# Attention times values for two batches in one run, in the first cross-attention of a six-phase kernel

## The chip, the cores and the metric

The kernel runs on one core of a Trainium2 chip as a single program. The metric is the device time of that program in microseconds, the median over its executions. It has five engines: TensorE (PE; its weight loads are listed as PEld), VectorE (DVE), ScalarE (ACT), GpSimd (POOL) and SyncE (SP), which issues the DMAs. All arithmetic in the stage treated here is in 32-bit floating point.

## The reference

A perceiver block of two layers on x (128 batches, 32 queries, 128 channels) and a context (128 batches, 257 keys, 128 channels). Each layer is cross-attention, self-attention and a feed-forward part, each with a layer norm before it and a residual sum after it. The change touches the first cross-attention only:

```python
q = split_heads(queries @ Wq + bq)      # 16 heads of 8 channels
k = split_heads(keys @ Wk + bk)
v = split_heads(values @ Wv + bv)
scores = jnp.einsum('bhqd,bhkd->bhqk', q, k) / jnp.sqrt(jnp.float32(HD))
scores = jnp.where(mask, jnp.float32(-1000000000000000.0), scores)
attn = jax.nn.softmax(scores, axis=-1)
ctx = jnp.einsum('bhqk,bhkd->bhqd', attn, v)
return ctx.reshape(b, sq, d) @ Wo + bo
```

The mask differs by batch. Queries are the normalised x, keys and values are both the context.

## The kernel before, in words

The six phases follow each other, each closed by a barrier. The first cross-attention is `phase_xattn0`. It prepares weights, query projections and the part of the last key (the 257th, held apart), and then walks over the 128 batches, one per **step**. A step g runs different stages of several batches, as a software pipeline written out by hand on each engine; `s.on(lag)` says whether batch g - lag exists. The first eight and last eight steps are unrolled, the others are a loop (`Fori`) of 8 steps per iteration, r = 0 to 7. The remainder r chooses the buffers. Engines meet through semaphores alone, each counting batches.

TensorE in step g (order of the code, `step` in the tensor block): scores of batch g (L552; four matmuls, one on each band of 32 rows of the array, to four PSUM banks); the projections of K (L529) and V (L534) for batch g+1 from the transposed context `cT`; at r % 4 = 1 the fold of the last key's part (L600); at r % 4 = 2 the output projection of a tile of four batches (L611, L613); the transposes of the probabilities of batch g-1, in two pairs of heads groups (L562, `turn_probs`); the transposes of the context of batch g+2 (L523, `turn`); the spread of the reciprocal sums of batch g-2 (L586, `spread_sums`); and attention times values for batch g-2 (L574, `values`): eight matmuls that the compiler issues as 16, side by side on four bands of 32 columns.

ScalarE in step g: the exponentials of batch g-1 (L684, four, each with a sum), the copies of K (L668) and V (L672) of batch g+1 out of PSUM, the copy of the first pair of transposed probabilities of g-1 (L692), the copy of the spread reciprocals of g-2 (L697, into `RS`). VectorE: masking and maximum of batch g (L731), the reciprocal (L751), the copy of the second pair of transposed probabilities (L755), the copy of the transposed context of g+2 (L719, `turned`), and the scaling of the result of `values` by `RS` into `OM` (L763). GpSimd prepares the mask and the block query of batch g+1 and small factors (L434 to L463). SyncE loads masks and context and stores the transposed context for the second layer (L408, L413).

The PSUM bank `b_vo` holds the projection of V in its first 256 columns and the result of `values` in the next 128; so the projection waits for the scaling of the batch before (`om_ok`), and `values` waits for the copy of V (`v_ev`). `V` has four buffers, `PT` (transposed probabilities) two, `RS` two. K's projection waits for the context copy of the step before (`ct_ev`), the second pair's transposes for all four exponentials (`e_ok`). In the listing, `one` and `run` set up a step; `fours` gives the tile number of a lag.

Of the kernel before, what the change touches and what calls it, by code (L numbers as in the profile page):

```python
# [19 lines left out]
ALU = mybir.AluOpType  # L20
# [5 lines left out]
P = 128  # L26
B = 128
SQ = 32
D = 128
# [272 lines left out]
def phase_xattn0(nc, sh, ctx_rows, mask, wq, bq, wk, bk, wv, bv, wo, bo):  # L302
    SCALE = HD0 ** -0.5
    with ExitStack() as ctx:
# [15 lines left out]
        Qb = sb("a_Qb", [D, 2, 4, SQ])  # L320
        cT = sb("a_cT", [D, 4, LAST])
        KT = sb("a_KT", [D, 2, SK])
        V = sb("a_V", [P, 4, 2, D])
        SM = sb("a_SM", [P, 2, 4, SK])
        PR = sb("a_PR", [P, 2, 4, SK])
        mx = sb("a_mx", [P, 2, 4])
# [5 lines left out]
        XL = sb("a_XL", [P, 2, 2 * BPT, 4, 4])  # L332
        LT = sb("a_LT", [P, BPT, SQ])
        VB = sb("a_VB", [P, 2, D])
        PT = sb("a_PT", [P, 2, 4, 2, P])
        RS = sb("a_RS", [P, 2, P])
        OM = sb("a_OM", [P, 2, 4, BPT, SQ])
        head4 = sb("a_head4", [D, 4])
# [35 lines left out]

        def run(eng, step, extra):

            def one(g, r, tile, fours):
                s = Step(g, r, B)
                s.tile, s.fours = tile, fours
                step(s)  # L380
            for g in range(8):
                one(g, g, g // 4, lambda lag, g=g: (g + lag) // 4)
            with eng.Fori(1, B // 8 - 1) as j:
                for r in range(8):
                    one(8 * j + r, r, 2 * j + r // 4, lambda lag, j=j, r=r: 2 * j + (r + lag) // 4)
            for g in range(B - 8, B + extra):
                one(g, g % 8, g // 4, lambda lag, g=g: (g + lag) // 4)

        @block.sync
        def _(sp):  # L390
# [106 lines left out]
        def _(pe):  # L497
# [25 lines left out]
                    last = nc.tensor.transpose(b_ck[:, c * P:(c + 1) * P], C[:, buf, c, :], sh.ident[:, :])  # L523
                last.then_inc(ct_ps, 1)

            def project(i, r):

                wait(pe, ct_ev, i + 1)
                nc.tensor.matmul(b_ck[:, LAST:2 * LAST], wk_s[:, :], cT[:, r % 4, :], start=True, stop=True  # L529
                                 ).then_inc(k_ps, 1)  # L530
                wait(pe, om_ok, i - 3)
                wait(pe, v_ev, i)
                for c in range(2):
                    last = nc.tensor.matmul(b_vo[:, c * D:(c + 1) * D], cT[:, r % 4, c * P:(c + 1) * P], wv_s[:, :],  # L534
                                            start=True, stop=True)
                last.then_inc(v_ps, 1)
# [27 lines left out]
                last.then_inc(pt_ps, 1)  # L564

            def values(s):
                g, v, par = s.g, (s.r - 2) % 4, s.r % 2
                wait(pe, pt0_ev, g - 1)
                wait(pe, pt1_ev, g - 1)
                wait(pe, v_ev, g + 2 if s.on(-1) else B)  # L570
                wait(pe, om_ok, g - 2)
                for c in range(2):
                    for hg in range(4):
                        last = nc.tensor.matmul(b_vo[32 * hg:32 * hg + 32, 2 * D:2 * D + P],  # L574
                                                V[:, v, c, 32 * hg:32 * hg + 32], PT[:, par, hg, c, :],
                                                start=(c == 0), stop=(c == 1), tile_position=(0, 32 * hg))
                last.then_inc(av_ps, 1)

            def spread_sums(s):

# [9 lines left out]
            def step(s):  # L590
                g, r = s.g, s.r
                if s.on(0):
                    scores(s)
                if s.on(-1):
                    project(g + 1, r + 1)
                if r % 4 == 1 and s.on(5):
                    wait(pe, x2_ok, 4 * s.fours(-5) + 4)
                    if s.on(0):
                        wait(pe, s_mx, 4 * g + 2)
                    nc.tensor.matmul(b_s[1][:, SPARE:SPARE + SQ],  # L600
                                     XL[:, (r - 5) // 4 % 2, :, :, :], sh.fold[:, :],
                                     start=True, stop=True).then_inc(l_ps, 1)
                if r % 4 == 2 and s.on(6):
                    wait(pe, om_ok, 4 * s.fours(-6) + 4)
                    wait(pe, l_ev, s.fours(-6) + 1)
                    pe.wait_ge(vb_in[(r - 6) // 4 % 2], s.values)
                    if s.on(0):
                        wait(pe, s_mx, 4 * g + 1)
                    tp = (r - 6) // 4 % 2
                    for h in range(4):  # L610
                        nc.tensor.matmul(b_s[0][:, SPARE:SPARE + D], OM[:, tp, h, :, :], wo_s[:, :],  # L611
                                         start=(h == 0), stop=False)
                    nc.tensor.matmul(b_s[0][:, SPARE:SPARE + D], LT[:, :, :], VB[:, tp, :], start=False, stop=True  # L613
                                     ).then_inc(y_ps, 1)
                if s.on(1):
                    turn_probs(s, 0)
                    turn_probs(s, 1)
                if s.on(-2):
                    turn(g + 2, (r + 2) % 4, s.ctx)
                if s.on(2):  # L620
                    spread_sums(s)
                    values(s)

            def one(g, r, tile, fours):
                s = Step(g, r, B)
                s.tile, s.fours = tile, fours
                s.ctx = 16 * (fours(2) + 1)
                s.values = 16 * (1 + (g - 6) // 8)
                step(s)

            turn(0, 0, 16)
            project(0, 0)
            turn(1, 1, 16)
            for g in range(8):
                one(g, g, g // 4, lambda lag, g=g: (g + lag) // 4)
            with pe.Fori(1, B // 8 - 1) as j:
                for r in range(8):
                    s = Step(8 * j + r, r, B)
                    s.tile, s.fours = 2 * j + r // 4, lambda lag, j=j, r=r: 2 * j + (r + lag) // 4
                    s.ctx = 32 * j + 16 * ((r + 2) // 4 + 1)  # L640
                    s.values = 16 * j if r < 6 else 16 * j + 16
                    step(s)
# [4 lines left out]
        def _(act):  # L647
# [17 lines left out]
            def project(i, r):  # L665
                wait(act, k_ps, i + 1)
                wait(act, s_ps, 4 * (i - 1))
                nc.scalar.activation(KT[:, r % 2, 0:LAST], b_ck[:, LAST:2 * LAST], ACT.Identity, bias=bias[:, 1:2]  # L668
                                     ).then_inc(k_ev, 1)
                wait(act, v_ps, i + 1)  # L670
                wait(act, av_ps, i - 3)
                nc.scalar.activation(V[:, r % 4, :, :].rearrange("p a d -> p (a d)"), b_vo[:, 0:2 * D],  # L672
                                     ACT.Copy).then_inc(v_ev, 1)

            def step(s):
                g, r = s.g, s.r
                par = r % 2
                if s.on(1):
                    wait(act, pt_ps, 2 * (g - 2))
                    wait(act, x2_ok, g - 2)  # L680
                    wait(act, rd_ok, g - 2)
                    wait(act, s_nmx, g)
                    for hg in range(4):
                        nc.scalar.activation(PR[:, 1 - par, hg, :], SM[:, 1 - par, hg, :], ACT.Exp,  # L684
                                             bias=nmx[:, 1 - par, hg:hg + 1],
                                             accum_out=den[:, 1 - par, hg:hg + 1]).then_inc(e_ok, 1)
                if s.on(-1):
                    project(g + 1, r + 1)
                if s.on(1):
                    wait(act, pt_ps, 2 * (g - 1) + 1)  # L690
                    wait(act, av_ps, g - 2)
                    nc.scalar.activation(PT[:, 1 - par, 0:2, :, :].rearrange("p a b c -> p (a b c)"), b_pt[0][:, :],  # L692
                                         ACT.Copy).then_inc(pt0_ev, 1)
                if s.on(2):
                    wait(act, r_ps, g - 1)
                    wait(act, om_ok, g - 3)
                    nc.scalar.activation(RS[:, par, :], b_s[2][:, SPARE:SPARE + P], ACT.Copy).then_inc(r_ev, 1)  # L697

            project(0, 0)
# [3 lines left out]
        def _(dve):  # L703
# [17 lines left out]
            def step(s):  # L721
# [29 lines left out]
                    nc.vector.reciprocal(rden[:, 1 - par, :], den[:, 1 - par, :]).then_inc(rd_ok, 1)  # L751
                if s.on(1):
                    wait(dve, pt_ps, 2 * g)
                    wait(dve, av_ps, g - 2)
                    nc.vector.tensor_copy(PT[:, 1 - par, 2:4, :, :].rearrange("p a b c -> p (a b c)"), b_pt[1][:, :]  # L755
                                          ).then_inc(pt1_ev, 1)
                if s.on(-2):
                    turned(g + 2, (r + 2) % 4, 16 * s.fours(2))
                if s.on(2):
                    wait(dve, av_ps, g - 1)  # L760
                    wait(dve, r_ev, g - 1)
                    wait(dve, y_ps, s.fours(-2) - 1)
                    nc.vector.tensor_tensor(OM[:, (r - 2) // 4 % 2, :, (r - 2) % 4, :],  # L763
                                            b_vo[:, 2 * D:2 * D + P].rearrange("p (h q) -> p h q", h=4),
                                            RS[:, par, :].rearrange("p (h q) -> p h q", h=4), ALU.mult).then_inc(om_ok, 1)

            turned(0, 0, 0)
            turned(1, 1, 0)
# [1873 lines left out]
```

## Time and profile before

| | us |
|---|---|
| median of 3 runs | 2544.7 |
| lowest, highest | 2540.48, 2546.29 |
| the profiled execution, its own time | 2540.67 |
| its span in the profile | 2538.9 |
| TensorE, VectorE, ScalarE, GpSimd busy in the span | 2126.7, 1645.4, 1443.1, 461.7 |
| granted TensorE clock, mean over the span | 0.922 |

The stage with the loop over batches lies between about 50 and 559 us of the span. A line of the profile names the engine, the source line and the tiles (output <- inputs, buffer numbers left out). "PE" times include the filling and emptying of the array, so neighbouring matmuls overlap in the listing; the distance between starts tells the pace. "Idle before" is the time in which that engine stood still in front of an instruction, followed by what ended it; "issue" there means that nothing the profile shows was waited for.

### The profile page before, as it was taken

Reading aid. Unit: us, or ns where it says so; the run is one execution under the profiler, and the core shown is the slowest. Engines: PE = TensorE matmul, PEld = TensorE weight load, DVE = VectorE, ACT = ScalarE, POOL = GpSimd, SP = SyncE. Lnnn points to the kernel's source line nnn. Section 1 sums busy time; section 2 is a strip of 40 time slices with the busy share of each in tenths; the row PEclk is TensorE's granted clock in tenths of the full one; section 3 lists DMA queues with packets and bytes.
Section 4 is the critical chain, followed back from the end, with each engine's and each line's share of the span. In section 5 each row is a group of like instructions: output and inputs, shape, how many; then the busy total and the mean of one; then the engine's idle time right before and its main releaser. Section 6 shows DMA issues by size and latency. Waiting matters only on the chain. (4 is left out here: it accounts for less than half of the span.)

```text
span 2538.9 us, 79619 instructions
## 1 busy us (share of the span) xinstructions
PE 2126.7 (84%) x26048; PEld 1642.3 (65%) x26087; DVE 1645.4 (65%) x5552; ACT 1443.1 (57%) x3655; POOL 461.7 (18%) x1109
## 2 busy tenths in 40 slices
PE   5999999988749997899999999996555035499998
PEld 3888888867636665899999999995144024344444
DVE  4777777776744444777787777786988888510110
ACT  4888888876612223555555555554777568522221
POOL 2555555533213331000000000000000120000000
PEclk9999999999959999999999999997988555799999
DMA  3222222210100001655555565552000000100001
GB/s 87 81 77 77 77 77 77 78 44 1 27 0 0 0 0 36 143 127 114 114 114 118 126 124 113 112 116 72 0 1 0 0 2 3 47 1 0 0 0 33
DMA packets 257633, 140.90 MB, mean 55 GB/s; under 512 B 40176, under 2 KB 255616, under 8 KB 257152
## 3 DMA queue, kind: packets, MB, share of 16 engines
q1 hardware_dynamic: 257536, 139.61, 23.5%
q8 instruction: 60, 0.98, 0.2%
q14 instruction: 37, 0.30, 0.0%
HBM read 118.57 MB, written 20.97 MB: 55 GB/s over the span
## 5 line engine op out<-in xcount | busy, mean ns | idle before, releaser
L1070 ACT ACTIVATE c_PR<-c_PR,c_nmx 128x257 f32<-128x257 f32 x512 | 252.7, 496 | 70.0 <-DVE c_nmx L1117 70.0
L1113 DVE CUSTOM_DVE_ANT_0 c_PR<-c_b,c_MB 128x257 f32<-128x257 f32 x512 | 194.9, 423 | 127.2 <-PE c_b L993 120.4
L684 ACT ACTIVATE a_PR<-a_SM,a_nmx 128x257 f32<-128x257 f32 x512 | 253.4, 500 | 4.0 <-POOL a_XL L459 3.6
L1004 PE MATMUL c_b<-c_PT,c_C 32*128 32x128 f32 x8192 | 239.3, 272 | 3.4 <-DVE c_PT L1130 2.1
L1004 PEld LDWEIGHTS c_b<-c_PT,c_C 32*128 32x128 f32 x8192 | 232.4, 187 | 7.5 <-issue 3.7
L993 PE MATMUL c_b<-c_cT,c_QP 128*128 128x257 f32 x1024 | 230.6, 383 | 1.3 <-ACT c_QP L1063 0.8
L731 DVE CUSTOM_DVE_ANT_0 a_SM<-a_bs,a_MB 128x257 f32<-128x257 f32 x512 | 188.0, 423 | 61.2 <-PE a_bs L552 33.5
L993 PEld LDWEIGHTS c_b<-c_cT,c_QP 128*128 128x128 f32 x1024 | 191.8, 190 | 32.1 <-issue 2.7
L1130 DVE STREAM_TRANSPOSE c_PT<-c_PR 128x256 f32<-128x256 f32 x512 | 181.3, 412 | 0.0
L1075 ACT ACTIVATE c_OT<-c_b 128x512 f32<-128x512 f32 x128 | 76.5, 598 | 168.8 <-PE c_b L1004 168.8
L2552 DVE TENSOR_TENSOR g_YS<-g_b,g_s 128x512 f32<-128x512 f32 x8 | 5.5, 692 | 224.2 <-PE g_b L2509 224.2
L1125 DVE TENSOR_SCALAR c_PR<-c_PR,c_rden 128x257 f32<-128x257 f32 x512 | 146.2, 351 | 4.5
L961 POOL TENSOR_TENSOR c_XL<-quarter,c_PR 128x16 f32<-128x16 f32 x128 | 27.8, 217 | 664.6 <-DVE c_PR L1125 664.6
L2520 ACT ACTIVATE g_A<-g_b,g_S 128x512 f32<-128x512 f32 x64 | 44.0, 687 | 170.7 <-PE g_b L2484 170.7
L562 PE MATMUL a_bp<-ident,a_PR 128*128 128x128 f32 x1024 | 134.5, 274 | 1.7 <-ACT a_PR L684 1.4
L2229 PE MATMUL d_bv<-d_WQ,d_HQ 128*128 128x512 bf16 x33 | 20.7, 633 | 129.0 <-PEq L2079 101.0
L978 PE MATMUL c_b<-c_XNT,c_A 128*128 (+1 forms) x1024 | 123.9, 280 | 5.7 <-POOL c_VB L967 5.7
L1023 PEld LDWEIGHTS c_b<-c_B,c_OT 128*128 128x128 f32 x1024 | 116.7, 192 | 15.9 <-DVE c_mx L1113 13.6
L1023 PE MATMUL c_b<-c_B,c_OT 128*128 128x128 f32 x1024 | 122.8, 278 | 4.5 <-DVE c_mx L1113 3.1
L978 PEld LDWEIGHTS c_b<-c_XNT,c_A 128*128 128x128 f32 x1024 | 118.8, 194 | 6.6 <-POOL c_VB L967 6.5
L1063 ACT ACTIVATE c_QP<-c_b 128x512 f32<-128x512 f32 x128 | 75.8, 597 | 76.5 <-PE c_b L978 76.5
L562 PEld LDWEIGHTS a_bp<-ident,a_PR 128*128 128x128 f32 x1024 | 117.0, 144 | 3.1 <-ACT a_PR L684 3.1
(487 smaller groups left out, 4923.8 us busy)
## 6 DMA issues: line engine op xcount, KB each, us to landing
c_C<-in_ctx_dram SPq DMA_DIRECT2D x512, 128.0 KB, 3.2
a_C<-in_ctx_dram SPq DMA_DIRECT2D x128, 128.0 KB, 2.1
ctxT_dram<-a_cT SPq DMA_DIRECT2D x128, 128.0 KB, 1.8
c_cT<-ctxT_dram SPq DMA_DIRECT2D x128, 128.0 KB, 3.3
a_MK<-in_mask_Bx1xSxS_bk_dram SPq DMA_DIRECT2D x128, 32.1 KB, 1.9
X<-in_x_dram SPq DMA_DIRECT2D x4, 512.0 KB, 6.2
g_h<-in_L_ffn_h_w_dram SPq DMA_DIRECT2D x2, 1024.0 KB, 8.3
out_dram<-X SPq DMA_DIRECT2D x1, 2048.0 KB, 8.7
```

What stands on the lines that cost most here:

```text
L562: last = nc.tensor.transpose(b_pt[pair][:, (2 * k + c) * P:(2 * k + c + 1) * P], PR[:, par, 2 * pair + k, c * P:(c + 1) * P], sh.ident[:, :])
L684: nc.scalar.activation(PR[:, 1 - par, hg, :], SM[:, 1 - par, hg, :], ACT.Exp, bias=nmx[:, 1 - par, hg:hg + 1], accum_out=den[:, 1 - par, h ...
L731: nc.vector.tensor_tensor_reduce(SM[:, par, hg, :], b_s[hg][:, 0:SK], MB[:, par, :], 1.0, NEG1, ALU.add, ALU.max, mx[:, par, hg:hg + 1]).t ...
L978: last = nc.tensor.matmul(banks[:, c, i * P:(i + 1) * P], A[:, 4 * c + i, :], sh.XNT[:, ds(tile * P, P)], start=True, stop=True)
L993: nc.tensor.matmul(banks[:, hg, 0:SK], QP[:, s.r, b, 4 * hg:4 * hg + 4, :], cT[:, buf, :], start=True, stop=True).then_inc(s_ps, 1)
L1004: last = nc.tensor.matmul(banks[:, h, 0:P], C[rows, b, kb, :], PT[rows, b, kb, :, :], start=(kb == 0), stop=(kb == NKB - 1), tile_position ...
L1023: nc.tensor.matmul(second[:, 0, 0:D], OT[:, par, h, :, :], BH[:, h, :], start=(h == 0), stop=False)
L1070: nc.scalar.activation(PR[:, b, hg, :], PR[:, b, hg, :], ACT.Exp, bias=nmx[:, b, hg:hg + 1], scale=SCALE, accum_out=den[:, b, hg:hg + 1]). ...
L1075: nc.scalar.activation(OT[:, par, :, b, :].rearrange("p (a h) q -> p h a q", h=4), banks[:, :, 0:P].rearrange("p h (a q) -> p h a q", a=4) ...
L1113: nc.vector.tensor_tensor_reduce(PR[:, b, hg, :], banks[:, hg, 0:SK], MB[:, :], 1.0, NEG1, ALU.add, ALU.max, mx[:, b, hg:hg + 1]).then_inc ...
L1125: nc.vector.tensor_scalar(PR[:, b, hg, :], PR[:, b, hg, :], rden[:, b, hg:hg + 1], None, ALU.mult).then_inc(n_ok, 1)
L1130: nc.vector.transpose(PT[:, b, :, hg, :], PR[:, b, hg, 0:LAST]).then_inc(t_ok, 1)
```

## The change

`values` is called in odd steps only (r % 2 = 1), and then for batches g-3 and g-2 one after the other: its output takes 256 columns of `b_vo` instead of 128, and the whole bank is then in use. VectorE scales both with one operation, which reads both buffers of `RS`. `om_ok` now counts pairs of batches, so that every wait on it is rewritten with `pairs(lag)` = (g + lag) // 2. `V` gets eight buffers for four and `PT` four for two, and the waits on `av_ps` that guard them are later by four and by two batches. The spread of the reciprocals stays in every step.

```diff
-        V = sb("a_V", [P, 4, 2, D])
+        V = sb("a_V", [P, 8, 2, D])
-        PT = sb("a_PT", [P, 2, 4, 2, P])
+        PT = sb("a_PT", [P, 4, 4, 2, P])
...
-            def project(i, r):
+            def project(i, r, pairs):
...
-                wait(pe, om_ok, i - 3)
+                wait(pe, om_ok, pairs)
...
             def values(s):
-                g, v, par = s.g, (s.r - 2) % 4, s.r % 2
+                g, r = s.g, s.r
                 wait(pe, pt0_ev, g - 1)
                 wait(pe, pt1_ev, g - 1)
                 wait(pe, v_ev, g + 2 if s.on(-1) else B)
-                wait(pe, om_ok, g - 2)
-                for c in range(2):
-                    for hg in range(4):
-                        last = nc.tensor.matmul(b_vo[32 * hg:32 * hg + 32, 2 * D:2 * D + P],
-                                                V[:, v, c, 32 * hg:32 * hg + 32], PT[:, par, hg, c, :],
-                                                start=(c == 0), stop=(c == 1), tile_position=(0, 32 * hg))
-                last.then_inc(av_ps, 1)
+                wait(pe, om_ok, s.pairs(-3))
+                for i in range(2):
+                    v, p = (r - 3 + i) % 8, (r - 3 + i) % 4
+                    for c in range(2):
+                        for hg in range(4):
+                            last = nc.tensor.matmul(b_vo[32 * hg:32 * hg + 32, 2 * D + i * P:2 * D + (i + 1) * P],
+                                                    V[:, v, c, 32 * hg:32 * hg + 32], PT[:, p, hg, c, :],
+                                                    start=(c == 0), stop=(c == 1), tile_position=(0, 32 * hg))
+                    last.then_inc(av_ps, 1)
...
-                    project(g + 1, r + 1)
+                    project(g + 1, r + 1, s.pairs(-2))
...
-                    wait(pe, om_ok, 4 * s.fours(-6) + 4)
+                    wait(pe, om_ok, 2 * s.fours(-6) + 2)
...
                 if s.on(2):
                     spread_sums(s)
+                if r % 2 == 1 and s.on(2):
                     values(s)
...
-                wait(act, av_ps, i - 3)
-                nc.scalar.activation(V[:, r % 4, :, :].rearrange("p a d -> p (a d)"), b_vo[:, 0:2 * D],
+                wait(act, av_ps, i - 7)
+                nc.scalar.activation(V[:, r % 8, :, :].rearrange("p a d -> p (a d)"), b_vo[:, 0:2 * D],
...
-                    wait(act, av_ps, g - 2)
-                    nc.scalar.activation(PT[:, 1 - par, 0:2, :, :].rearrange("p a b c -> p (a b c)"), b_pt[0][:, :],
+                    wait(act, av_ps, g - 4)
+                    nc.scalar.activation(PT[:, (r - 1) % 4, 0:2, :, :].rearrange("p a b c -> p (a b c)"), b_pt[0][:, :],
...
-                    wait(act, om_ok, g - 3)
+                    wait(act, om_ok, s.pairs(-2))
...
-                    wait(dve, av_ps, g - 2)
-                    nc.vector.tensor_copy(PT[:, 1 - par, 2:4, :, :].rearrange("p a b c -> p (a b c)"), b_pt[1][:, :]
+                    wait(dve, av_ps, g - 4)
+                    nc.vector.tensor_copy(PT[:, (r - 1) % 4, 2:4, :, :].rearrange("p a b c -> p (a b c)"), b_pt[1][:, :]
...
-                if s.on(2):
+                if r % 2 == 1 and s.on(2):
+                    b = (r - 3) % 4
                     wait(dve, av_ps, g - 1)
                     wait(dve, r_ev, g - 1)
                     wait(dve, y_ps, s.fours(-2) - 1)
-                    nc.vector.tensor_tensor(OM[:, (r - 2) // 4 % 2, :, (r - 2) % 4, :],
-                                            b_vo[:, 2 * D:2 * D + P].rearrange("p (h q) -> p h q", h=4),
-                                            RS[:, par, :].rearrange("p (h q) -> p h q", h=4), ALU.mult).then_inc(om_ok, 1)
+                    nc.vector.tensor_tensor(OM[:, (r - 2) // 4 % 2, :, b:b + 2, :],
+                                            b_vo[:, 2 * D:2 * D + 2 * P].rearrange("p (b h q) -> p h b q", b=2, h=4),
+                                            RS[:, :, :].rearrange("p b (h q) -> p h b q", h=4), ALU.mult
+                                            ).then_inc(om_ok, 1)
```

## Rows read from the trace of the kernel before

**Rows 1.** Busy time by stretch: the stage, and one iteration of its loop.

```profile
core 0: us, PE busy (x) PEld busy (x) DVE busy (x) ACT busy (x) POOL busy (x), PEclk, DMA share, GB/s
52.00:548.00 496.00, 494.29 (x5490) 397.08 (x5489) 395.13 (x1728) 432.83 (x1508) 258.86 (x659) 1.00 0.27 77
269.82:301.54 31.72, 31.66 (x353) 25.51 (x353) 25.22 (x111) 27.59 (x97) 16.49 (x43) 1.00 0.26 77
```

**Rows 2.** Waits, 100 to 500 us: us in total, times, longest us.

```profile
PEld a_bck L529 <- issue: 33.4, 100, 0.3
ACT a_PT L692 <- PE a_bp L562: 28.5, 38, 1.0
...
PEld a_bs L552 <- issue: 21.7, 101, 0.3
...
ACT a_RS L697 <- PE a_bs L586: 17.7, 100, 0.2
```

**Rows 3.** Timeline of TensorE, spread to spread in a plain step: start, duration, line.

```profile
285.04 0.27 PE L586 MATMUL a_bs<-ident,a_m 128*128 128x128 f32 x1
...
285.24 0.65 PE L574 MATMUL a_bvo<-a_PT,a_V 128*32 128x128 f32 x16
...
285.81 0.76 PE L552 MATMUL a_bs<-a_KT,a_Qb 32*128 32x257 f32 x8
...
286.50 0.70 PE L529 MATMUL a_bck<-a_cT,a_wk 128*128 128x256 f32 x2
...
287.03 0.61 PE L534 MATMUL a_bvo<-a_wv,a_cT 128*128 128x128 f32 x4
...
287.48 1.04 PE L562 MATMUL a_bp<-ident,a_PR 128*128 128x128 f32 x8
...
288.35 0.38 PE L523 MATMUL a_bck<-ident,a_C 128*128 128x128 f32 x2
...
288.57 0.27 PE L586 MATMUL a_bs<-ident,a_m 128*128 128x128 f32 x1
```

**Rows 4.** Timeline of VectorE and ScalarE around the first of these spreads.

```profile
285.02 0.69 DVE L755 COPY a_PT<-a_bp 128x512 f32<-128x512 f32 x1
...
285.34 0.28 ACT L697 ACTIVATE a_RS<-a_bs 128x128 f32<-128x128 f32 x1 [0.17 <-PE a_bs L586]
...
285.52 0.50 ACT L684 ACTIVATE a_PR<-a_SM,a_nmx 128x257 f32<-128x257 f32 x1
285.62 0.41 DVE L719 COPY a_cT<-a_bck 128x256 f32<-128x256 f32 x1
...
285.96 0.28 DVE L763 TENSOR_TENSOR a_OM<-a_bvo,a_RS 128x128 f32<-128x128 f32 x1
```

**Rows 5.** Timeline of TensorE in the first steps: scores straight after context transposes.

```profile
52.94 0.41 PE L523 MATMUL a_bck<-ident,a_C 128*128 128x128 f32 x2 [0.17 <-issue]
...
53.27 0.80 PE L552 MATMUL a_bs<-a_KT,a_Qb 32*128 32x257 f32 x8
```

**Rows 6.** Timeline at the stage's end, last exponentials but one, and last values.

```profile
550.74 0.50 ACT L684 ACTIVATE a_PR<-a_SM,a_nmx 128x257 f32<-128x257 f32 x1
...
552.86 0.66 PE L562 MATMUL a_bp<-ident,a_PR 128*128 128x128 f32 x4 [0.33 <-ACT a_PR L684]
...
553.35 0.27 PE L586 MATMUL a_bs<-ident,a_m 128*128 128x128 f32 x1
...
556.64 0.69 DVE L755 COPY a_PT<-a_bp 128x512 f32<-128x512 f32 x1 [0.54 <-PE a_bp L562]
...
557.80 0.64 PE L574 MATMUL a_bvo<-a_PT,a_V 128*32 128x128 f32 x16
```

**Rows 7.** Timeline of TensorE at the loop's start, r = 0, and r = 1.

```profile
301.54 1.15 PE L552 MATMUL a_bs<-a_KT,a_Qb 32*128 32x257 f32 x8
302.62 0.70 PE L529 MATMUL a_bck<-a_cT,a_wk 128*128 128x256 f32 x2
...
304.69 0.27 PE L586 MATMUL a_bs<-ident,a_m 128*128 128x128 f32 x1
...
306.23 0.70 PE L529 MATMUL a_bck<-a_cT,a_wk 128*128 128x256 f32 x2
...
308.57 0.27 PE L586 MATMUL a_bs<-ident,a_m 128*128 128x128 f32 x1
```

More of the change, by code:

```diff
@@ L375, in run, with one @@
         def run(eng, step, extra):
-            def one(g, r, tile, fours):
+            def one(g, r, tile, fours, pairs):
                 s = Step(g, r, B)
-                s.tile, s.fours = tile, fours
+                s.tile, s.fours, s.pairs = tile, fours, pairs
                 step(s)
             for g in range(8):
-                one(g, g, g // 4, lambda lag, g=g: (g + lag) // 4)
+                one(g, g, g // 4, lambda lag, g=g: (g + lag) // 4, lambda lag, g=g: (g + lag) // 2)
             with eng.Fori(1, B // 8 - 1) as j:
                 for r in range(8):
-                    one(8 * j + r, r, 2 * j + r // 4, lambda lag, j=j, r=r: 2 * j + (r + lag) // 4)
+                    one(8 * j + r, r, 2 * j + r // 4, lambda lag, j=j, r=r: 2 * j + (r + lag) // 4,
+                        lambda lag, j=j, r=r: 4 * j + (r + lag) // 2)
             for g in range(B - 8, B + extra):
-                one(g, g % 8, g // 4, lambda lag, g=g: (g + lag) // 4)
+                one(g, g % 8, g // 4, lambda lag, g=g: (g + lag) // 4, lambda lag, g=g: (g + lag) // 2)
         @block.sync
@@ L628, in one @@
                 s.values = 16 * (1 + (g - 6) // 8)
+                s.pairs = lambda lag: (g + lag) // 2
                 step(s)
             turn(0, 0, 16)
-            project(0, 0)
+            project(0, 0, 0)
             turn(1, 1, 16)
@@ L639, in _ @@
                     s.tile, s.fours = 2 * j + r // 4, lambda lag, j=j, r=r: 2 * j + (r + lag) // 4
+                    s.pairs = lambda lag, j=j, r=r: 4 * j + (r + lag) // 2
                     s.ctx = 32 * j + 16 * ((r + 2) // 4 + 1)
```

## The prediction

> **What bounds the kernel now.** I read the busy time by stretch first. In the first cross-attention (52 to 548 us) TensorE is busy 494.3 of 496 us at a granted clock of 1.00, ScalarE 432.8, VectorE 395.1 [rows 1]. One iteration of the loop, 8 batches, takes 31.72 us, 3.97 a batch. A busy TensorE is not yet one that never waits, so the list of waits comes next: between 100 and 500 us the others wait for TensorE or for each other, ScalarE for the transposed probabilities and for the spread sums (L692, L697), while the only large waits in front of TensorE's loads are put down to "issue", 0.33 us a step before the projection of K (L529) and 0.2 before scores [rows 2]. The order of TensorE's work in one plain step (r = 4) then shows that nothing is late: spread, 0.20, values, 0.57, scores, 0.69, K, 0.53, V, 0.45, probabilities, 0.87, context, 0.22, next spread, in all 3.53 us [rows 3]. TensorE sets the step.
>
> But the others follow close behind [rows 4]. After the spread (285.04) ScalarE copies it (285.34) and starts the four exponentials at 285.52, 0.48 us after the spread. VectorE copies the probabilities at 285.02 and the context after them, from 285.62 to 286.03, 0.99 after the spread; TensorE wants that copy for K at 286.50. So the margin for K is 0.47 us. The exponentials are done 2.12 us after their start (below), at 287.64, and the second pair's transposes come 0.44 after 287.48, at 287.92: 0.28 us. They matter, because the 0.57 us of values lies just between the spread and scores.
>
> **What the change saves on TensorE.** Both sizes of the multiplication stay, and so does its count. What goes is one change of the array's layout in two steps: spread to values costs 0.20, where one matmul follows another of its kind in 0.11 (turn to spread, two matmuls in 0.22) [rows 3]. A run of values is 0.37 us to its last group of four plus 0.20 for the change to scores. A second batch behind the first adds four groups of 0.11, 0.44. An odd step therefore grows by 0.44 and an even one loses 0.57, if scores follow a spread as they follow values. That passage is not in the steady steps, but in the first ones scores follow a context transpose: 52.94 to 53.27, of which one matmul is 0.11, so 0.2 again [rows 5]. By TensorE alone a pair of steps gains 0.13 us; 64 pairs, 8.3 us. The Trainium skill says of this (TensorEngine Tiling (Array Packing), Key Properties) that a change of mode, not of tile, drains the engine; the 0.20 against 0.11 agrees, and by that rule the second batch's run pays no drain of its own, as the sum has it.
>
> **What it loses: two floors behind the even steps.** Call S the start of a spread in an even step.
> K of the next step needs VectorE's context copy, which ends at S+0.99 and cannot move, as it follows the transposes, not the values [rows 4]. With 0.04 for the signal (the spread ends at 285.31, its copy starts at 285.34) K starts at S+1.04 at the earliest. TensorE would be there at S+0.20+0.69 = S+0.89. So 0.15 of the 0.57 is not gained.
> The second pair's transposes need all four exponentials. These start at S+0.48, and the tail, where TensorE waits for them openly, gives the rest: exponentials from 550.74, transposes at 552.86, 2.12 later; spread at 553.35, 0.49 after those transposes [rows 6]. So the transposes come at S+2.60 or later, and with the context's 0.22 the next spread is at S+3.31 or later. By the K floor alone it would be 1.04+0.53+0.45+0.87+0.22 = 3.11; by TensorE's work alone 2.96.
>
> There are four even-to-odd passages in eight steps. Two (r = 2 and 6) lead to plain steps: 3.53 before, 3.31 after, 0.22 gained. Two (r = 0 and 4) lead to steps with the fold matmul (L600), which lies in front of the transposes and covers the second floor. There K to the next spread takes 306.23 to 308.57, 2.34, so S+1.04+2.34 = 3.38, against 304.69 to 308.57, 3.88, before: 0.50 gained, since K's floor also swallows a slower scores run (spread to K is 1.54 here, 1.46 in the plain step) [rows 3, 7]. The four odd-to-even passages each lose 0.44. Eight steps: 4 x 0.44 - 2 x 0.50 - 2 x 0.22 = **+0.32 us**, and 16 times that is +5.1 us.
>
> **The other edits.** The scaling on VectorE becomes one operation of 256 elements for two of 128. One took 0.28 [rows 4]; the double one lies between 0.28 and the 0.41 of the 256-element context copy, and I take 0.41. It starts about where it did relative to scores (285.96), ends 0.13 later, and who waits for it, V of the next step (287.03), has 0.66 us left: nothing. Queued behind it on VectorE is the first masking, which waits for scores anyway. The copy of the sums on ScalarE in an even step now waits for the scaling of the step before, over two us earlier: nothing. Deeper buffers for values and probabilities lift waits on L574 that do not appear among the waits [rows 2]; they are needed as values are consumed later, and they gain nothing. If that cover went, a wait of ScalarE on values would push the exponentials directly, the second floor. The output projection's wait now counts pairs and falls on the same scaling as before. SyncE's and POOL's work and order stay. At the end of the stage batch 126 is multiplied together with 127: the pair can start when VectorE's copy from 556.64 has ended (557.33), and with 0.44 more ends about when the last run from 557.80 ends now; the longer scaling leaves +0.2 us [rows 6].
>
> Sum: +5.3 us. The profiled execution took 2540.67 (span 2538.9); it would take 2546.0. It lies 4.0 below the median of the runs shown, 2544.7, which becomes **2550.0**. About 0.2%, 5.1 us, is what a measurement of this kernel can tell from no change.
>
> **The rivals.**
> *TensorE alone decides (faster).* If context copy and exponentials are early enough after all, each pair gains its 0.13: -8.3+0.2 = -8.1, 2536.6. For it: a full TensorE and no wait of it on either today [rows 2]. Against it: the margins of rows 3 and 4. It decides from the point where K can start by S+0.89 and the second transposes by about S+2.4. Chance 0.20.
> *Only the K floor (no change).* If the exponentials get ahead, for instance because ScalarE's copy of the sums comes sooner, r = 2 and 6 give 3.53-3.11 = 0.42: 1.76-1.00-0.84 = -0.08 in eight steps, -1.3+0.2, 2543.6. Chance 0.15.
> *TensorE's instruction stream loses its lead (clearly slower).* A double run is 64 instructions in a row, loads and matmuls. At the loop's start, where the stream was interrupted, scores to K takes 301.54 to 302.62, 1.08 instead of 0.69 [rows 7]. Were every scores run after a double one like that, it would be 0.39 x 64 = 25 us more: 2575. Against it: after a run of 32 it never happens inside an iteration. 
>
> **How the numbers follow.** The forecast has 0.55, its own range is 2544 to 2557: 0.05 us on K's signal is 3 us over 64 pairs, and 0.1 on the exposed weight load before the late transposes another 3; the scaling, at 0.28 or 0.41, moves nothing. Above the bound of 2549.8 lies a little over half of it, 0.31; 0.24 is within. The one-floor case goes to "same" (0.15), TensorE alone to faster (0.20), the lost lead to slower (0.07); 0.03 remains for the unknown, 0.01 faster and 0.02 slower. So faster 0.21, same 0.39, slower 0.40. The range takes in TensorE alone at the bottom and ends above the forecast's own: 2536 to 2558; the lost lead stays outside.
>
> **What would show it.** In the changed kernel: even-to-odd spreads 3.38 and 3.31 apart, odd-to-even ones 0.44 longer than now; L529 waiting 0.15 us for the context copy of VectorE in every odd step; L562 waiting for ScalarE's exponentials at r = 3 and 7 only; a TensorE busy for less than 99% of the stage; one iteration of 32.0 us instead of 31.7. I am wrong if even-to-odd spreads are 2.96 apart (TensorE alone), or if scores to K takes over 1 us in even steps (lead lost).

## The result and the profile after

The changed kernel takes **2562.27 us** (median of 6 runs, 2559.15 to 2567.48), the kernel before, on the same chip, 2540.82 (6 runs, 2540.04 to 2546.29): a ratio of 1.008 [1.0066, 1.0094], slower by 21.5 us. The forecast was slower by 5.3, 2550.0 in a range of 2536 to 2558. The direction was the likeliest of the three, the size was a quarter of the real one, and the time lies outside the range. The profiled execution took 2562.98 us (span 2561.2, clock 0.919) against 2540.67 (2538.9, 0.922).

The busy time by stretch of the changed kernel, for the stage and for one iteration of its loop, as in [rows 1]:

```profile
core 0: us, PE busy (x) PEld busy (x) DVE busy (x) ACT busy (x) POOL busy (x), PEclk, DMA share, GB/s
52.00:564.00 512.00, 511.47 (x5433) 414.14 (x5433) 394.39 (x1654) 440.05 (x1498) 256.02 (x654) 1.00 0.26 75
276.63:309.69 33.06, 33.06 (x354) 26.81 (x353) 25.37 (x107) 28.25 (x97) 16.44 (x43) 1.00 0.25 73
```

An iteration takes 33.06 us instead of 31.72. 1.34 more, 16 times (14 iterations of the loop, and two more for the unrolled first and last eight steps), is 21.4 us: the whole difference lies in this stage. The granted clock is 1.00 in both. TensorE reads as busy in all 33.06 us, more than before, although the same matmuls are done. Nothing here looks like a wait, and the list of waits of the changed kernel (100 to 500 us: us in total, times, longest) is hardly louder than [rows 2]:

```profile
PEld a_bck L530 <- issue: 32.3, 97, 0.3
PEld a_bs L553 <- issue: 30.1, 144, 0.3
...
ACT a_RS L703 <- PE a_bs L589: 16.1, 85, 0.2
```

Of the lines for TensorE's loads only the second grew: waits before loads of scores, 144 instead of 101. Scores are one run per step and there are some 97 steps in the window, so about half the steps now have a second gap inside the run of scores. The timeline of one even step (r = 0) of the changed kernel, TensorE's matmuls and loads, ScalarE and VectorE together, shows it:

```profile
313.97 0.27 PE L589 MATMUL a_bs<-ident,a_m 128*128 128x128 f32 x1
...
314.05 0.69 DVE L761 COPY a_PT<-a_bp 128x512 f32<-128x512 f32 x1 [0.34 <-PE a_bp L563]
314.17 0.30 PEld L553 LDWEIGHTS a_bs<-a_KT,a_Qb 32*128 32x128 f32 x4 [0.17 <-issue]
314.17 1.41 PE L553 MATMUL a_bs<-a_KT,a_Qb 32*128 32x257 f32 x8
314.36 0.28 ACT L703 ACTIVATE a_RS<-a_bs 128x128 f32<-128x128 f32 x1 [0.17 <-PE a_bs L589]
314.54 0.51 ACT L690 ACTIVATE a_PR<-a_SM,a_nmx 128x257 f32<-128x257 f32 x1
314.65 0.41 DVE L725 COPY a_cT<-a_bck 128x256 f32<-128x256 f32 x1
314.75 0.43 PEld L553 LDWEIGHTS a_bs<-a_KT,a_Qb 32*128 32x128 f32 x4 [0.28 <-issue]
...
315.51 0.30 PEld L530 LDWEIGHTS a_bck<-a_cT,a_wk 128*128 128x128 f32 x2 [0.33 <-issue]
```

Scores start 0.20 after the spread, as forecast. But their eight loads, one row of 0.31 in other steps, are two rows of four, and the second begins at 314.75, 0.11 after ScalarE's copy of the sums (314.36 + 0.28 = 314.64) has ended. Two loads belong to each head group, so the second four are groups 2 and 3, counted from 0. The code says why: `if hg == 2: wait(pe, r_ev, g - 2)`. The spread of the reciprocals is written into spare columns of the bank of the third head group, `b_s[2]`, and scores may not write that bank before ScalarE has read the sums (L703). Before, the 0.57 us of values lay between the two and hid the copy, all but a few hundredths of a us (the part on the prediction has them). The four head groups, which side by side take 0.65 to 0.69, now run in two halves, and K starts at 315.51, 1.54 after the spread and 0.87 after the end of the copy.

A busy TensorE hides this. In the profile, where the ends of matmuls are modelled, the four matmuls of the first half last from 314.17 to 314.87, 0.70 us, and the second half's loads begin at 314.75, before that end. There is no hole between the halves, only a long row: 1.41 us for eight matmuls that take 0.76 in [rows 3].

The rest of TensorE's order, from this even step over the next odd one to the next even one, answers to [rows 3, 7]:

```profile
316.05 0.61 PE L535 MATMUL a_bvo<-a_wv,a_cT 128*128 128x128 f32 x4
316.49 0.31 PE L603 MATMUL a_bs<-fold,a_XL 128*128 128x32 f32 x2
316.63 1.07 PE L563 MATMUL a_bp<-ident,a_PR 128*128 128x128 f32 x8
317.54 0.38 PE L524 MATMUL a_bck<-ident,a_C 128*128 128x128 f32 x2
317.76 0.27 PE L589 MATMUL a_bs<-ident,a_m 128*128 128x128 f32 x1
317.96 1.08 PE L577 MATMUL a_bvo<-a_PT,a_V 128*32 128x128 f32 x32
318.97 0.72 PE L553 MATMUL a_bs<-a_KT,a_Qb 32*128 32x257 f32 x8
319.62 0.70 PE L530 MATMUL a_bck<-a_cT,a_wk 128*128 128x256 f32 x2
```

After the double run (317.96 to 318.97, 1.01 instead of 0.57) everything follows without a gap. The next passage from an even to an odd step, r = 2, a plain one:

```profile
322.81 0.27 PE L589 MATMUL a_bs<-ident,a_m 128*128 128x128 f32 x1
323.01 1.33 PE L553 MATMUL a_bs<-a_KT,a_Qb 32*128 32x257 f32 x8
324.27 0.70 PE L530 MATMUL a_bck<-a_cT,a_wk 128*128 128x256 f32 x2
...
326.34 0.27 PE L589 MATMUL a_bs<-ident,a_m 128*128 128x128 f32 x1
```

Spread to K is 1.46 here, spread to spread 3.53: to the hundredth what it was before with 0.57 us more work in between [rows 3]. The even step gives nothing back here, and 0.09 at r = 0 (3.79 against 3.88 in [rows 7]); odd steps pay 0.40.

### The profile page after: what moved, and what is told of

It reads as the page before. It is cut to its first block and busy times, and to the rows that moved or that the text cites. A ratio compares the mean times of both kernels' runs of the same rounds, so it can differ in the third digit from the quotient of the medians.

```text
span 2561.2 us, 79424 instructions
## 1 busy us (share of the span) xinstructions
PE 2153.6 (84%) x26048; PEld 1668.9 (65%) x26087; DVE 1647.4 (64%) x5488; ACT 1453.6 (57%) x3655; POOL 460.4 (18%) x1109
## 5 line engine op out<-in xcount | busy, mean ns | idle before, releaser
L553 PE MATMUL a_bs<-a_KT,a_Qb 32*128 32x257 f32 x1024 | 138.4, 425 | 0.0
```

The source lines that it names most:

```text
L553: nc.tensor.matmul(b_s[hg][:, 0:SK], Qb[rows, par, :, :], KT[rows, par, :], start=True, stop=True, tile_position=(32 * hg, 0)).then_inc(s_ ...
```

## The experiments

Theory A throughout is the bank: the third head group waits for the copy of the sums. Each ratio is against the kernel before, run beside it.

**1 and 2. Give the copy time, or give it another bank.** Both start from the changed kernel.

```
                     turn_probs(s, 1)
-                if s.on(-2):
-                    turn(g + 2, (r + 2) % 4, s.ctx)
                 if s.on(2):
                     spread_sums(s)
+                if s.on(-2):
+                    turn(g + 2, (r + 2) % 4, s.ctx)
```

> The changed kernel with one order turned round on TensorE: the spread of the reciprocals goes ahead of the context transposes. Theory A (the bank wait): scores of the third group of heads go to the PSUM bank that still holds the spread, so they wait for ScalarE's copy of it, which ends 0.67 us after the spread's start; K then starts at 1.54 after the spread instead of the 0.89 I had forecast. With the spread 0.22 us earlier K of an odd step comes 0.22 earlier: 64 x 0.22 = 14 us faster than the changed kernel, about 2548. Theory B (K waits for VectorE's context copy, as I had forecast): the context transposes come 0.11 later and nothing is gained, 2562. Theory C (TensorE's instruction stream has lost its lead): the order does not matter, 2562.

```
-                    if hg == 2:
+                    if hg == 3:
                         wait(pe, r_ev, g - 2)
...
-                    wait(pe, s_mx, 4 * s.g + 3)
+                    wait(pe, s_mx, 4 * s.g + 4)
...
-                nc.tensor.transpose(b_s[2][:, SPARE:SPARE + P],
+                nc.tensor.transpose(b_s[3][:, SPARE:SPARE + P],
```

> The changed kernel with the spread in the fourth scores bank instead of the third, and the wait before the fourth group of heads. Theory A: the third group is free, the fourth is held as long as the third was, one group less is behind the wait: K 0.13 us earlier in odd steps, 64 x 0.13 = 8 us, about 2554. Theories B and C: no difference, 2562.

Measured: 2549.94, 1.0028 [1.0019, 1.0038], and 2556.7, 1.006 [1.0043, 1.0077]. By the two medians the context transposes as cover are worth 12 us (14 expected). Loads and releases of x1 in an even step, whose spread is at 252.64:

```profile
252.95 0.28 ACT L703 ACTIVATE a_RS<-a_bs 128x128 f32<-128x128 f32 x1
253.06 0.71 PEld L553 LDWEIGHTS a_bs<-a_KT,a_Qb 32*128 32x128 f32 x8 [0.17 <-issue]
...
254.10 0.30 PEld L530 LDWEIGHTS a_bck<-a_cT,a_wk 128*128 128x128 f32 x2 [0.33 <-DVE a_cT L725]
```

K is again at the end of the copy + 0.87 (253.23 and 254.10), spread to K again 1.46. The last line names VectorE's context copy as what K waited for, but in this trace that copy ran from 253.45 for 0.41 us and so had ended 0.24 before K, where a K that really waits for it starts 0.05 to 0.06 after it (experiment 5); theory B does not hold here. What is saved is that the 0.22 of the context transposes now lies inside that time. The fourth bank gains 5.6 us by the medians against 8 expected, with four runs and an interval that overlaps that of the changed kernel. Its trace has the expected size: behind the spread of a step r = 2 scores start at 255.07 and K at 256.20, 1.13 where the changed kernel has 1.26, and behind the other even steps 1.20 or 1.21 where it has 1.34. The loads split there as six and two instead of four and four.

**3. Take the cover from the kernel before.** No second batch, no double scaling; values go ahead of the spread in every step.

```
                 if s.on(2):
-                    spread_sums(s)
                     values(s)
+                    spread_sums(s)
```

> The kernel before with values of each step ahead of the spread, so that scores follow the spread in every step and nothing covers ScalarE's copy. One batch per run, as before. Theory A: K 1.54 us after the spread in every step instead of 0.89: 0.65 a step plus one more change of the array's layout, 0.1 to 0.2: 126 steps, 80 to 105 us slower than before, 2620 to 2645. Theory B: only the context copy counts, which comes at the same distance from its transposes: one more change of layout, 2555 to 2565. Theory C (the double run is what hurts): there is no double run, the same 2555 to 2565.

Measured: 2627.52, 1.0334 [1.0317, 1.0351], 85 us slower. The same mechanism in a kernel without the change, now in every step that has a spread:

```profile
252.25 0.30 PEld L552 LDWEIGHTS a_bs<-a_KT,a_Qb 32*128 32x128 f32 x4
252.36 0.28 ACT L697 ACTIVATE a_RS<-a_bs 128x128 f32<-128x128 f32 x1 [0.89 <-PE a_bs L586]
...
252.75 0.43 PEld L552 LDWEIGHTS a_bs<-a_KT,a_Qb 32*128 32x128 f32 x4 [0.20 <-issue]
253.51 0.30 PEld L529 LDWEIGHTS a_bck<-a_cT,a_wk 128*128 128x128 f32 x2 [0.33 <-issue]
```

Copy ends 252.64, second half 0.11 later, K 0.87 later. 85 us over 128 steps is 0.67 a step. Not all of it is the bank. A plain step grows from 3.53 to 4.26 us: scores to K takes 1.26 instead of 0.69, 0.57 more, and the other 0.16 lies in front of scores, where the new order has one more change of the array's layout (context to scores, with spread and values between them, takes 1.15 instead of 0.99). This is the strongest run of the study: most of the loss appears without a second batch in the run and without the double scaling.

**4. Cover it twice over.** From the changed kernel, the spread goes between the two pairs of transposes of probabilities, so that the second pair and the context's transposes lie behind it.

```
                     turn_probs(s, 0)
+                if s.on(2):
+                    spread_sums(s)
+                if s.on(1):
                     turn_probs(s, 1)
                 if s.on(-2):
                     turn(g + 2, (r + 2) % 4, s.ctx)
-                if s.on(2):
-                    spread_sums(s)
```

> The changed kernel with the spread between the two pairs of probability transposes, 0.66 us earlier on TensorE. Theory A: the wait is now set by ScalarE's own order, since its copy of the first pair (0.60) stands ahead of the copy of the sums: if it follows after 0.5 us the sums come 0.27 earlier than now, if after the 0.76 seen in all steps not at all. So it lies between 2541 and 2562, and below x1 only in the first case. Theories B and C: 2562.

Measured: 2545.3, 1.0013 [1.0003, 1.0023]: 17 of the 21 us are gone. Behind even steps scores to K still takes 0.96 to 1.06. Between 200 and 270 us K starts there 0.88 to 0.94 after the end of the copy of the sums and 0.05 to 0.10 after VectorE's context copy: the two waits end almost together, so this run alone does not tell them apart. The next one does.

**5. Copy the sums ahead of the probabilities on ScalarE**, on top of 4.

```
+                if s.on(2):
+                    wait(act, r_ps, g - 1)
+                    wait(act, om_ok, s.pairs(-2))
+                    nc.scalar.activation(RS[:, par, :], b_s[2][:, SPARE:SPARE + P], ACT.Copy).then_inc(r_ev, 1)
                 if s.on(1):
...
                                          ACT.Copy).then_inc(pt0_ev, 1)
-                if s.on(2):
-                    wait(act, r_ps, g - 1)
...
```

> The changed kernel with the spread between the two pairs of probability transposes, and ScalarE's copy of the sums ahead of its copy of the first pair. Theory A (bank wait first, the context copy next): in the run with the spread between the pairs K of the odd step starts 0.05 us after VectorE's context copy has ended, in the passages read, so the bank wait is no longer the last; an earlier copy of the sums gains next to nothing, 2541 to 2546. Theory A' (the bank wait is the only one): it goes as well, each even-to-odd passage falls to TensorE's own 2.96 us in plain steps, 2529 to 2535.

Measured: 2544.89, 1.001 [1.0001, 1.0019]; no gain over x4. The wait stands open in the timeline now:

```profile
243.13 0.28 ACT L699 ACTIVATE a_RS<-a_bs 128x128 f32<-128x128 f32 x1 [0.16 <-PE a_bs L589]
...
243.60 0.76 PE L553 MATMUL a_bs<-a_KT,a_Qb 32*128 32x257 f32 x8
244.19 0.41 DVE L726 COPY a_cT<-a_bck 128x256 f32<-128x256 f32 x1
244.66 0.30 PEld L530 LDWEIGHTS a_bck<-a_cT,a_wk 128*128 128x128 f32 x2 [0.71 <-DVE a_cT L726]
```

The copy of the sums ended before scores even began, the scores are not split, and K waits for the context copy, which ends at 244.60, 0.06 before it, and stands behind the copy of probabilities on VectorE. K now starts over 1.1 us after the copy of the sums: this is the K floor of the prediction.

**6. Lift that too**, on top of 5: VectorE copies the context ahead of its probabilities.

```
+                if s.on(-2):
+                    turned(g + 2, (r + 2) % 4, 16 * s.fours(2))
                 if s.on(1):
...
                                           ).then_inc(pt1_ev, 1)
-                if s.on(-2):
-                    turned(g + 2, (r + 2) % 4, 16 * s.fours(2))
```

> As the run before it, and VectorE copies the transposed context ahead of the second pair of probabilities. Theory A: K can start 0.89 us after the second pair's transposes have ended, where TensorE comes at 1.10, so the second floor is gone too; what remains is some 0.12 us for the exponentials at r = 3 and 7. In eight steps of the loop four even-to-odd passages lose 0.57, two of them 0.12 less, and three of the odd-to-even ones pay 0.40, one 0.24 as measured in the changed kernel: -2.28+0.24+1.44 = -0.6, 16 times that about -10 us against the kernel before, 2532. A rival: that ScalarE has become the bound, then it stays at 2541 to 2546.

Measured: 2545.06, 1.0011 [1.0002, 1.002]: not the 2532 of theory A, a miss. K does start 0.69 after scores. But the next thing in TensorE's order is late now:

```profile
259.46 0.76 PE L553 MATMUL a_bs<-a_KT,a_Qb 32*128 32x257 f32 x8
259.57 0.42 DVE L726 COPY a_cT<-a_bck 128x256 f32<-128x256 f32 x1 [0.44 <-PE a_bck L524]
...
260.68 0.61 PE L535 MATMUL a_bvo<-a_wv,a_cT 128*128 128x128 f32 x4
261.33 0.30 PEld L603 LDWEIGHTS a_bs<-fold,a_XL 128*128 128x128 f32 x2 [0.23 <-DVE a_mx L738]
```

The fold matmul writes spare columns of `b_s[1]` and waits for VectorE to mask the scores in it (L738); it follows V by 0.65 instead of 0.44. Once more it is a shared bank. The list of waits between 100 and 500 us has 25 such waits of the fold (7.0 us) and 25 of the spread for the same masking (7.1 us).

**7. The same three changes of order with one batch at a time**, from the kernel before. On TensorE:

```
                     turn_probs(s, 0)
+                if s.on(2):
+                    spread_sums(s)
+                if s.on(1):
                     turn_probs(s, 1)
...
                 if s.on(2):
-                    spread_sums(s)
                     values(s)
```

On ScalarE and VectorE the moves are those of 5 and 6.

> The kernel before with the same three changes of order (spread between the pairs, the sums and the context copied earlier) and values of one batch in every step. It tells what the order alone is worth. Theory A: the kernel before has no wait in these places, since values cover them, so nothing is gained, 2540 to 2545, and the difference to the run before it, about 10 us, is the gain of running two batches together. Rival: the order brings the gain by itself, about 2532.

Measured: 2543.28, 1.0006 [0.9997, 1.0015]. With this order two batches in a run (6) gain nothing over one (7), where TensorE's own count gives 8.3 us.

**8. Is the longer scaling part of it?** The changed kernel with two scalings of 128 elements in place of one of 256.

```
-                    nc.vector.tensor_tensor(OM[:, (r - 2) // 4 % 2, :, b:b + 2, :], ...
+                    for k in range(2):
+                        last = nc.vector.tensor_tensor(OM[:, (r - 2) // 4 % 2, :, b + k, :], ...
```

> The changed kernel with two scaling operations of 128 elements instead of one of 256. All theories: VectorE waits for scores behind it and has 0.6 us to spare, so 2562 as the changed kernel. If it is slower by 5 us or more, the scaling is on the path and my step on it was wrong.

Measured: 2563.09, 1.0083 [1.0068, 1.0099], as the changed kernel. The scaling is not on the path.

**9 and 10. Move the fold as well.** x9 is x6 with the fold matmul after the first pair of transposes; x10 the same from x7, one batch at a time.

```
-                if r % 4 == 1 and s.on(5):
-                    wait(pe, x2_ok, 4 * s.fours(-5) + 4)
...
                     turn_probs(s, 0)
+                if r % 4 == 1 and s.on(5):
+                    wait(pe, x2_ok, 4 * s.fours(-5) + 4)
```

> The run with both floors lifted, and in addition the fold matmul (once in four steps, odd ones) after the first pair of probability transposes. In that run scores to K was down to 0.69 in even-to-odd passages, but the fold waited for VectorE's masking, 0.65 and 0.75 us from V to it instead of 0.44, and the second pair waited 0.2 for the exponentials at r = 3 and 7. Theory A (each shortened passage runs into the next engine): the fold's wait goes, 0.5 us in eight steps, 8 us in all; the exponentials' wait stays: 2537, some 5 us below the kernel before. Rival: VectorE is the bound in odd steps, the wait only moves to the transposes or the masks, 2542 to 2546.

> The same order of all work, fold included, with values of one batch in every step. In the run with this order and the fold in its old place V to fold was 0.54 instead of 0.44, so 0.2 us in eight steps can go, 3 us: 2539 to 2542. The difference to the run before it is what two batches in a run bring when the order suits them: by theory A 2 to 5 us in their favour, by the rival none or against them.

Measured: x9 **2534.49**, 0.9976 [0.9967, 0.9985], and x10 2537.72, 0.9985 [0.9976, 0.9994]. Both beat the kernel before, x9 beats all. By the medians, 3.2 us are the worth of two batches in a run. The two intervals against the kernel before overlap, but the two kernels ran on the same chip, 11 times each, and x9 is the faster in 108 of the 121 pairs of runs: the sign is clear, the size is not. An even step of x9:

```profile
199.76 0.76 PE L553 MATMUL a_bs<-a_KT,a_Qb 32*128 32x257 f32 x8
200.45 0.70 PE L530 MATMUL a_bck<-a_cT,a_wk 128*128 128x256 f32 x2
...
202.08 0.14 PEld L589 LDWEIGHTS a_bs<-ident,a_m 128*128 128x128 f32 x1 [0.29 <-DVE a_mx L738]
```

Scores to K is 0.69. What is left is the spread, which waits up to 0.29 in every fourth step for the masking of its own bank (7.4 us in 26 waits between 100 and 500 us), a wait that x10 does not list. That is likely where the rest of the 8.3 us by TensorE's count went, but no run took the wait away.

**11. Put one suspect back.** x9 with the move of 5 undone: ScalarE copies probabilities first and the sums after them, as in the changed kernel.

```
-                if s.on(2):
-                    wait(act, r_ps, g - 1)
...
                                          ACT.Copy).then_inc(pt0_ev, 1)
+                if s.on(2):
+                    wait(act, r_ps, g - 1)
...
```

> As the run with the fold later, but ScalarE copies the first pair of probabilities ahead of the sums again. The exponentials of the next step start after both; 0.1 us earlier in this order, since the copy of the sums has to wait for the spread. Theory A: the exponentials' wait at r = 3 and 7 falls by 0.1, but the sums end 0.4 later and the bank wait of the third group of heads comes back with 0.1 to 0.3 in four passages of eight steps: 5 to 15 us slower than the run with the fold later. If the bank wait were harmless here it would be 2 to 4 us faster.

Measured: 2542.66, 1.0008 [0.9999, 1.0018]: the order of two copies on ScalarE alone costs 8.2 us in x9, within the 5 to 15 expected. In its trace between 200 and 270 us K behind every even step starts 0.87 or 0.88 after the end of the copy of the sums, and 0.35 to 0.44 after that of the context: the bank's wait is back, and nothing else is near.

**12. The deeper buffers alone**, in the kernel before, with waits that match.

```
-        V = sb("a_V", [P, 4, 2, D])
+        V = sb("a_V", [P, 8, 2, D])
...
-        PT = sb("a_PT", [P, 2, 4, 2, P])
+        PT = sb("a_PT", [P, 4, 4, 2, P])
...
-                wait(act, av_ps, i - 3)
+                wait(act, av_ps, i - 7)
```

> The kernel before with the deeper buffers alone (eight for values, four for probabilities, their waits later). All theories: no wait on values is visible before, nothing changes, 2540 to 2545.

Measured: 2542.94, 1.0008 [0.9998, 1.0017]. No effect clear of noise.

## Why the prediction was wrong in size

The direction came out as forecast, but not by the forecast's mechanism: the wait that costs the time is not in the sum, and both waits that are in it did not bind. That the sign was right is partly luck. Taken by its own steps:

- **What bounds the kernel**: right in the main. TensorE sets the step; others are close behind it. The margins listed there were K's and the exponentials'. A third was missing, and it was used up. In [rows 3, 4] the copy of the sums ends at 285.34 + 0.28 = 285.62, and 0.87 later is 286.49; K starts at 286.50. The kernel before already stood at this wait: between 100 and 500 us K starts 0.87 to 0.91 after the end of that copy in 86 of some 100 steps (nearly all the others are the first of an iteration, where scores themselves come late), and scores to K takes 0.68 to 0.77 in them. Where the copy ends over 0.6 us before scores start, in odd steps of the changed kernel and in x7 and x10, it takes 0.64 or 0.65 in nearly every step, the first of an iteration again left out. The longer scores run of [rows 7], read there as a slower run, is the same thing:

```profile
305.08 0.28 ACT L697 ACTIVATE a_RS<-a_bs 128x128 f32<-128x128 f32 x1 [0.25 <-PE a_bs L586]
...
305.47 0.84 PE L552 MATMUL a_bs<-a_KT,a_Qb 32*128 32x257 f32 x8
```

  The copy ends at 305.36 and K starts at 306.23, 0.87 later. The cover of values was not 0.57 us with room to spare; it was short by some 0.04 to 0.12, an estimate from 0.69 and 0.77 against 0.65; the row of the eight loads of scores, 0.35 at 285.81 and 0.43 at 305.46 where it is 0.31 with an early copy, says the same. The prediction also passed over one line of the list of waits, 16.8 us in 100 waits of L574 for ScalarE's copy L692. That one is harmless: in x7 the same 0.17 a step stands there as "issue".
- **TensorE's count**: right. A change of layout costs 0.20 and stayed so; a second batch adds 0.44 to values (0.57 to 1.01). After a double run scores take 0.65 instead of 0.69, so an odd step costs 0.40, not 0.44: the longer run of values gives the copy of the sums more cover (x7 and x10 have the 0.65 with one batch in a run). The Trainium skill (TensorEngine Tiling (Array Packing), Key Properties) ties the drain to a change of mode, and the two batches of a run have the same; the trace agrees: 32 matmuls went from 317.96 to 318.97 in one row, 0.44 more than 16.
- **"TensorE would be there at S+0.20+0.69 = S+0.89"**: this is the step that failed. S+0.20 held; the 0.69 did not. And it was tied to **"the copy of the sums on ScalarE … nothing"**, where I had asked what that copy waits for and not who waits for the copy. Scores' third group does. The true earliest K is the end of the copy + 0.87, S+1.46 to S+1.54, in place of S+1.04.
- **The K floor**: it is real (x5: K 0.05 to 0.06 after the context copy; for the signal 0.04 was taken where 285.31 to 285.34 is 0.03), but it came behind the bank's wait and did not bind in the changed kernel, where K starts 0.44 or more after that copy.
- **The exponentials' floor**: never reached in the loop of the changed kernel, since everything behind K came later; the lists of waits of x6 and x9 name none of TensorE for the exponentials either. TensorE waits for the masking there.
- **The sum**: four odd-to-even passages were forecast at +0.44; three measured +0.40 and the one across the loop's end +0.24, together 1.44 (forecast 1.76). Even-to-odd at r = 0 and 4, in the iteration from 276.63 to 309.69: gain 0.09 each, forecast 0.50. At r = 2 it is 3.54, as before, and at r = 6 3.61, a loss of 0.08; forecast a gain of 0.22 each. In all 1.44 - 0.18 + 0.08 = 1.34, as by the windows; forecast 0.32. The mis-sized term is the even-to-odd gain: 1.44 us an iteration promised, 0.10 delivered.
- **Scaling, buffers, order of SyncE and POOL**: nothing, right (x8, x12). The double scaling measured 425 ns (taken as 0.41):

```profile
L703 ACT ACTIVATE a_RS<-a_bs 128x128 f32<-128x128 f32 x97 | 26.9, 277 | 17.2 <-PE a_bs L589 16.1
...
L770 DVE TENSOR_TENSOR a_OM<-a_bvo,a_RS 128x256 f32<-128x256 f32 x48 | 20.4, 425 | 16.5 <-PE a_bvo L577 16.5
```

- **The lost-lead rival** (2575): wrong. Its sign, scores to K above 1 us behind even steps, did appear, from another cause: the second half of the scores starts 0.11 after the end of ScalarE's copy in the timelines of two kernels, and scores right after the 64 instructions take 0.65, as in x7 after 32. Of the Trainium skill's 64 places (Advanced Engine Details and Errata, Engine Queue Depths) no run here shows an effect. That the sign I had named could be met by two causes was a fault of the test; where the gap lies inside the run tells them apart.
- **"A TensorE busy for less than 99% of the stage"** as a test: wrong, 511.47 of 512.

## What to carry to other kernels

Work between a write to a PSUM bank and the next use of that bank is cover for the copy that empties it. Before moving it away, look up every wait that names the bank, spare columns included, and put down the end of the copy plus the time to the next instruction as a floor. One lifted wait is not a gain as long as the next engine's floor lies just below it: here the order had to be changed in four places (spread, ScalarE's copies, VectorE's copies, fold) before two batches in a run paid, and then by about 3 of 2540 us against one batch in the same order, and 7 against the kernel before.

## What was not expected of the hardware

Four scores of 32 rows each run side by side in 0.65 to 0.69 us; held up in the middle, the second half alone takes 0.76 to K, so a late bank costs more than the time by which it is late: the second half began 0.58 after the first, and the run became 1.34 where unsplit scores need 0.69, 0.65 more. And TensorE's busy time rose to 33.06 of 33.06 us while in every second step half of its scores were held up: the duration of a matmul row in the timeline (1.41 against 0.76), a load row split in two, and the count of waits that comes of that split (144 against 101) were the places to see it. A wait can also be there without any of these signs. Before the change K followed the copy of the sums by the same 0.87 us in nearly every step, with one row of eight loads, 0.04 to 0.12 longer and without a gap; it is the constant distance between the two that gives it away.
